# Attention: both heads' probabilities transposed together behind the scores, in two 64-row tiles

## What is computed

```python
x = x + tanh(g_xattn) * xattn(layernorm(x), ctx, ctx)
# xattn(q, k, v):
qh, kh, vh = split_heads(q @ Wq), split_heads(k @ Wk), split_heads(v @ Wv)
dots = where(mask | causal, -max, einsum('bhid,bhjd->bhij', qh, kh) * SCALE)
out = einsum('bhij,bhjd->bhid', softmax(dots), vh)
return merge_heads(out) @ Wo + bo
```

## Time and profile before

| what | value |
|---|---|
| median of 3 runs | 1721.62 us (1720.88 to 1722.0) |
| the profiled execution | 1721.11 us, span 1719.3 us |
| mean granted clock of PE | 0.982 of full speed |
| PE busy | 1641.4 us (95%), 13700 matmul records |
| DVE busy | 1354.0 us (79%) |
| ACT busy | 1157.7 us (67%) |
| POOL busy | 491.0 us (29%) |
| transposes of probabilities on PE (L792) | 1024, 160.3 us busy |
| exponentials on ACT (L428) | 1024, 396.9 us busy |

### The profile page before, as it was taken

How to read it: one execution, slowest core, us unless ns; L and a number is a source line. 1 busy time by engine, 2 the same in 40 slices (tenths; PEclk the granted TensorE clock), 3 DMA queues, 4 the chain that set the end, 5 groups by cost and what they waited for, 6 DMA issues and landing times. The chain is left out here.

```text
span 1719.3 us, 39257 instructions
## 1 busy us (share of the span) xinstructions
PE 1641.4 (95%) x13700; PEld 1371.8 (80%) x13700; DVE 1354.0 (79%) x2305; ACT 1157.7 (67%) x3047; POOL 491.0 (29%) x367
## 2 busy tenths in 40 slices
PE   8999999999999999999999999989997998886998
PEld 6788888888888888888888888778775777775887
DVE  7767778677686786777767768876887999898997
ACT  5666666566666665666666666557665999796665
POOL 2322323323232232232332323320001765560000
PEclk9999999999999999999999999998998999997999
DMA  4210001101010010100110001018994886564664
GB/s 140 70 40 27 24 26 37 38 26 37 14 50 24 26 37 25 39 24 26 37 38 26 24 26 37 14 62 250 332 320 179 300 295 230 214 251 172 214 220 152
DMA packets 74783, 177.18 MB, mean 103 GB/s; under 512 B 19312, under 2 KB 49136, under 8 KB 71792
## 3 DMA queue, kind: packets, MB, share of 16 engines
q1 hardware_dynamic: 74736, 176.57, 30.0%
HBM read 96.86 MB, written 76.02 MB: 101 GB/s over the span
## 5 line engine op out<-in xcount | busy, mean ns | idle before, releaser
L386 POOL TENSOR_TENSOR prob<-prob,rsums 128x512 f32<-128x512 f32 x254 | 266.9, 1051 | 785.0 <-DVE rsums L582 642.3
L428 ACT ACTIVATE prob<-masked,neg_max 128x128 f32<-128x128 f32 x1024 | 396.9, 392 | 77.6 <-DVE neg_max L560 76.7
L428 ACT ACTIVATION_READ_ACCUMULATOR prob<-masked,neg_max 128x1 f32 x1024 | 196.0, 191 | 0.0
L560 DVE TENSOR_REDUCE neg_max<-masked 128x4 f32<-128x512 f32 x254 | 174.4, 686 | 8.8
L578 DVE COPY probT<-trans 128x512 f32<-128x512 f32 x126 | 86.9, 690 | 110.0 <-PE trans L792 107.1
L558 DVE TENSOR_TENSOR masked<-score,mask_add 128x512 f32<-128x512 f32 x254 | 172.9, 681 | 0.8
L792 PE MATMUL trans<-ident,prob 128*128 128x128 f32 x1024 | 160.3, 279 | 0.8 <-POOL prob L406 0.8
L443 ACT ACTIVATE qT<-proj 128x512 f32<-128x512 f32 x128 | 76.7, 600 | 111.1 <-PE proj L757 111.1
L840 PE MATMUL y<-wo_hi,o_hi 128*128 128x256 f32 x508 | 145.9, 287 | 2.1 <-DVE wo_lo L508 2.0
L813 PEld LDWEIGHTS pv<-probT,v_sb 128*64 128x64 f32 x2048 | 109.7, 136 | 46.4 <-issue 44.4
L813 PE MATMUL pv<-probT,v_sb 128*64 128x128 f32 x2048 | 140.1, 279 | 6.6 <-issue 5.9
(11 more groups left out here) (251 smaller groups left out, 4386.5 us busy)
## 6 DMA issues: line engine op xcount, KB each, us to landing
gate<-gate_d SPq DMA_DIRECT2D x30, 768.0 KB, 4.3
n_x<-n_x_d SPq DMA_DIRECT2D x25, 512.0 KB, 5.0
gate_d<-stage SPq DMA_DIRECT2D x8, 1536.0 KB, 5.5
n_u_d<-w_raw SPq DMA_DIRECT2D x16, 768.0 KB, 4.0
stage<-n_u_d SPq DMA_DIRECT2D x16, 768.0 KB, 6.1
gate_d<-gate SPq DMA_DIRECT2D x7, 1536.0 KB, 5.5
x_in<-in_x SPq DMA_DIRECT2D x16, 512.0 KB, 4.0
ctx_in<-in_ctx SPq DMA_DIRECT2D x16, 512.0 KB, 3.5
```

The costliest lines, as they stand in the source:

```text
L386: gp.tensor_tensor(pr, pr, rsums[:, h, :].rearrange("p (b o) -> p b o", o=1).broadcast_to([P, NB, P]), ALU.mult).then_inc(normed, 1)
L428: nc.scalar.activation(prob[:, c % 2, h, b, :], masked[:, h, b, :], ACT.Exp, bias=neg_max[:, h, b:b + 1], accum_out=psums[:, h, b:b + 1]). ...
L560: nc.vector.tensor_reduce(neg_max[:, h, :], masked[:, h], X, ALU.max, negate=True).then_inc(max_done, 1)
```

## The change

Both heads' probabilities of a pair are transposed together, in front of the step's query product. Each 128x128 transpose becomes two: rows 0 to 63 of the probabilities go to the bank `trans`, rows 64 to 127 to the `proj` bank whose turn it is, so the turn is a new kind of job in `jobs`. One bank then holds half of the query rows of both heads, and ACT copies both banks, one after the other; DVE has no such copy any more. In steps 2 to 6 ACT takes both heads' exponentials before it copies the keys; in steps 0, 1 and 7 the order stays. DVE inverts the second head's sums right after the copies of the values. The feed-forward weights at the end have three banks in place of four.

```diff
+    V_JOBS = [(0, 1), (2, 3), (4,), (5,), (6,), (7,), (), ()]
     for c in range(NC):
-        jobs += [(c, "q", 0)]
+        jobs += [(c, "turn", 0), (c, "q", 0)]
...
 # ACT
+            K_COPY_FIRST = (0, 1, NC - 1)
+            def copy_turned(u, b, before):
+                act.wait_ge(transposed, u + 1)
+                wait(act, pv_done, u)
+                nc.scalar.activation(probT[:, :, :, 0:HALF], halves(hand.banks[0]), ACT.Copy).then_inc(first_copied, 1)
+                act.wait_ge(projected[b], before + 1)
+                nc.scalar.activation(probT[:, :, :, HALF:P], halves(proj[b]), ACT.Copy).then_inc(copied[b], 1)
...
                 if soft:
                     exps(u - 1, c + 1, 0)
+                    if c not in K_COPY_FIRST:
+                        exps(u - 1, c + 1, 1)
...
-                if soft:
+                if soft and c in K_COPY_FIRST:
                     exps(u - 1, c + 1, 1)
...
 # DVE
-                if old:
-                    dve.wait_ge(transposed, 2 * (u - 2) + 2)
-                    wait(dve, pv_done, u - 2)
-                    nc.vector.tensor_copy(probT[:, 1], trans[:]).then_inc(probT_copied[1], 1)
...
 # PE
+            def transpose_prob(u, c, b, before):
+                pe.wait_ge(normed, 2 * u + 2)
+                wait(pe, first_copied, u)
+                wait(pe, copied[b], before)
+                pe.nop(nofuse=True)
+                to = [halves(a) for a in (hand.banks[0], proj[b])]
+                for e in range(NB):
+                    for h in range(2):
+                        for r in range(2):
+                            rows = slice(r * HALF, (r + 1) * HALF)
+                            last = nc.tensor.transpose(to[r][:, h, e, :], prob[rows, c % 2, h, e, :], ident[rows, rows])
+                            if e == NB - 1 and h == 1:
+                                last.then_inc(projected[b] if r else transposed, 1)
...
                 if old:
-                    transpose_prob(u - 2, co, 0)
+                    transpose_prob(u - 2, co, *turn_bank(g, c, u))
...
-                if old:
-                    transpose_prob(u - 2, co, 1)
...
-        ffn_banks = [proj[0][:], proj[1][:]] + [a[:].rearrange("p b q -> p (b q)") for a in score]
+        ffn_banks = [proj[1][:]] + [a[:].rearrange("p b q -> p (b q)") for a in score]
```

More of the change, by code:

```diff
@@ L111, in jobs_of, with turn_job @@
         return [(i, n) for i, (cc, k, n) in enumerate(jobs) if cc == c and k == kind]
+    no_turn = [jobs.index((c, "turn", 0)) for c in range(2)]
+    no_input = [i for i, (_, kind, _) in enumerate(jobs) if kind == "t"]
     def nth(g, i):
-        skipped = KC // 2 if isinstance(g, int) and g == G - 1 and i == last_k else 0
-        return i % 2, (FIRST + i) // 2 + (NJ // 2) * g - skipped
+        left_out = [a for a in no_turn if not isinstance(g, int) or g > 0 or g == 0 and a < i]
+        if isinstance(g, int) and g >= G - 1:
+            left_out += [a for a in no_input if g == G or a < i]
+        return i % 2, (FIRST + i) // 2 + (NJ // 2) * g - sum(a % 2 == i % 2 for a in left_out)
+    def turn_job(u):
+        if not isinstance(u, int):
+            return None
+        if u >= U:
+            b, before = nth(G, 0)
+            return b, before + u - U
+        return nth(u // NC, jobs_of(u % NC, "turn")[0][0])
     with ExitStack() as st:
@@ L276, in w_part, with turn_bank @@
             return a[n][:].rearrange("p (k n) -> p k n", k=KC if n < 3 else 1)[:, :, lo:hi]
+        def turn_bank(g, c, u):
+            return turn_job(u) if isinstance(u, int) else nth(g, jobs_of(c, "turn")[0][0])
         def staged(i):
@@ L422, in exps @@
             def exps(u, c, h):
-                wait(act, transposed, 2 * (u - 2) + h + 1)
+                wait(act, transposed, u - 1)
                 act.wait_ge(max_done, 2 * u + h + 1)
@@ L434, in step @@
                 if old:
-                    act.wait_ge(transposed, 2 * (u - 2) + 1)
-                    wait(act, pv_done, u - 2)
-                    nc.scalar.activation(probT[:, 0], trans[:], ACT.Copy).then_inc(probT_copied[0], 1)
+                    copy_turned(u - 2, *turn_bank(g, c, u))
                 if new:
@@ L588, in step @@
                         nc.vector.tensor_copy(v_sb[:, n % NB, cols], proj[b][:]).then_inc(copied[b], 1)
+                if soft:
+                    dve.wait_ge(exp_done, NB * (2 * (u - 1) + 2))
+                    wait(dve, normed, 2 * (u - 1))
+                    nc.vector.reciprocal(rsums[:, 1, :], psums[:, 1, :]).then_inc(recip_done, 1)
                 if nxt:
@@ L801, in scores_free, with times_v @@
                     wait(pe, masked_done, 2 * (u - 1) + h + 1)
-            def times_v(u, c, then=None):
-                for h in range(2):
-                    pe.wait_ge(probT_copied[h], u + 1)
+            def times_v(u, c, b, before, then=None):
+                pe.wait_ge(first_copied, u + 1)
+                pe.wait_ge(copied[b], before + 1)
                 wait(pe, out_split, u)
@@ L884, in step @@
                 if nxt:
+                    transpose_in(g, *ts[2])
                     transpose_in(g, *ts[3])
                 if old:
-                    times_v(u - 2, co, (g, c, u) if new else None)
+                    times_v(u - 2, co, *turn_bank(g, c, u), (g, c, u) if new else None)
                 if new:
```

76 lines of the change are left out of this document (24 added, 52 removed).

## The result

The changed kernel takes 1790.57 us (median of 4 runs, 1786.75 to 1794.18), the kernel before 1721.25: the ratio is 1.0404 [1.0379, 1.0429]. The direction and its mechanism came as predicted. The range of 1742 to 1795 holds the time, but the forecast of 1761 was 30 us short. The profiled execution took 1792.12, its span 1790.3.

The account below looks back on a forecast made before the run. A step was taken to last as long as TensorE's matmuls, other engines having slack. Step changes of +38 and 2 at the end made +40 on 1721.1, forecasting 1761 us, range 1742 to 1795.

Parts of the forecast that it names:

- rival A: In the turn, the two row tiles do not overlap or weight loads set the pace: 1810 us, chance 0.13.
- The turn's price: On TensorE the tiled turn takes 0.64 us instead of 0.88, so a step with nobody late is 0.24 shorter.
- Steps 1 to 3: Loop steps where the turn waits 0.20 us for GpSimd's second multiplication against 0.24 saved: -0.04 each.
- Step 0: First loop step: the turn waits 0.86 us for GpSimd behind the second head's late exponentials: +0.62.
- Step 4: Loop step with late exponentials: eight stand before the keys' copy, so the next scores come later: +1.12 us.
- step 6: Loop step without a value product to hide the turn's wait; eight exponentials and the keys' copy delay scores: +0.91 us.
- Step 5: Loop step given time by the pushed-back one before it, the keys just fitting: -0.24 us.
- Step 7: Last loop step, held by ScalarE behind the second input transpose, before which the turn is 0.20 us longer: +0.20.
- The sum over the attention: All loop steps' changes over the 16 groups, added together: +38 us.
- The tail: End of the attention: two copies in a row and three feed-forward banks cost 0 to 3 us, taken as 2.
- Rival C: The keys' copies are not late in steps four and six but the waits stay: 1722 us, no difference, chance 0.05.
- Rival B: GpSimd's second multiplication ends before the scores in all steps and the keys fit: faster, 1690 us, chance 0.06.

## Why the prediction was right, and where it was off

- **What bounds.** Right: a step lasts as long as its matmuls until somebody is late, and the change makes two late. Alone, in the kernel before, the order of ScalarE costs 37 us; in the changed kernel the reciprocal's move gave back 25. No run undoes both, so that the two add up is not shown.
- **The range** holds the time by luck. Its part above 1780 stood for a part of rival A, a pair of transposes at 0.085; the pair came at 0.062. What filled the 30-odd us above the forecast was the term below on how late a result is taken up (17), the first and last groups (4), the tail (2) and the stages behind (8).
- **The turn's price** was right: 0.24 saved. The steps of 8.22 that have no wait show it, and with it the waits account for the others, to 0.05.
- **Steps 1 to 3** were put at -0.04 and came at +0.04, +0.14, +0.07. The step that failed is "TensorE takes up such a result 0.06 after its end", which I had read at one place, the end of the attention. In front of the turn it is 0.15, in step 2 0.24, and so the wait is 0.29 (0.39 in step 2) instead of 0.20. Why it differs is open: the new `transpose_prob` has one wait more and an empty instruction behind the wait for GpSimd, and no run takes them out.
- **Step 0**: +0.82 for +0.62, the same term. GpSimd ends 0.86 after the turn could have begun, foreseen as 0.80, and the release is 0.24.
- **Step 4**: +1.25 for +1.12, **step 6** +1.07 for +0.91. The chain is as written: exponentials, keys, last block, scores. From the end of the keys' copy to the scores it took 0.60, and 0.71 in the run of this order alone, where I had 0.43: the same 0.06 again, for ScalarE's copy. Why the exponentials of step 4 come late was read loosely: the 0.57 us sum began before GpSimd's add had ended, and no run tests whether the add holds it up. The sum used only their start.
- **Step 5**: -0.10 for -0.24. "The keys just fit" was 0.14 short, by the same term: their copy ends at 661.58 and the scores come 0.59 later. **Step 7**: +0.27 for +0.20.
- **The sum over the attention** was +38 and came to +58.6. The measured step lengths, at the counts of the prediction, make 17 of the 21 missing; the rest lies in the first and last groups.
- **The tail**, taken as 2, was 6.8 at the gate stage's first instruction and 3.8 by its second tile. The step that failed is the sentence that put the three banks at "between 0 and 3 (28 closing transposes of 0.11 come behind a later one)": it followed TensorE's order, not VectorE's, where the fourth low part stands behind the maxima, and it kept 0.11 for transposes behind a hole in which the granted clock fell.
- **"The later stages are not touched"**: no line is, yet they were 8.2 longer in the profile. That term was set to nothing without a row behind it, and its cause is open.
- **Rival A** is out by the order of rows: the tiles overlap. The argument against it from the loads was misread: only the first two of four whole transposes' loads start 0.06 apart. All four take 0.42 and one 0.14, so the other two distances are 0.11:

```profile
611.79 0.42 PEld L792 LDWEIGHTS trans<-ident,prob 128*128 128x128 f32 x4
...
628.26 0.14 PEld L811 LDWEIGHTS trans<-ident,prob 64*128 64x128 f32 x1
...
628.29 0.14 PEld L811 LDWEIGHTS proj<-ident,prob 64*128 64x128 f32 x1
```

  (The last two are of the changed kernel.) The Trainium skill's page "TensorE: Matmul & The Clock Gate", section "LDWEIGHTS (loading the stationary operand)", would have a load of 128 columns take 107 ns. The whole transposes' 0.11 agrees with it; in the turn the two 64-row tiles' loads of 128 columns start 0.03 apart (0.06 within a tile), so there the measurement decides against it. **Rival C** fell with its condition: the keys were late. **Rival B** did not come: GpSimd ends after the scores, because the change leaves the reciprocal behind the values' copy. Moved in front of it, the reciprocal does let the turn follow the scores in steps 1 to 4.
- **The rule on changing the tiling**: the Trainium skill's page "TensorEngine Tiling (Array Packing)", section "Tiling Modes", has a change drain the engine. The runs fit it: the same tiles that save 0.2 a step next to the scores save next to nothing between two full-array products.

## What to carry to other kernels

Work on the busiest engine that is moved to an earlier place saves its own time only if what it consumes is there by then: look for what released the producer (here a reciprocal behind a copy that had nothing to do with it), and price the release by several places of the trace, not by the shortest. When two consumers of one engine's output both sit without slack, an order that helps one takes from the other; then move the consumer behind work that covers it, and check that the added copy fits there. A bank taken away at a stage's end is paid where another engine's queue releases it, and, if TensorE idles for it, in its clock as well.

## What was not expected

- The same kind of release took 0.06 at one place, 0.15 or 0.24 from GpSimd in front of the turn, and 0.23 or 0.34 from ScalarE's copy of the keys.
- Two 64-row tiles with 64 moving columns give a pair every 0.062 us, and keep overlapping where the program lists one tile after the other: spread 0.76, not the 0.93 of 15 x 0.062.
- 5.42 us of nothing on TensorE are followed by 5.4 us at a granted clock of 0.59; 1.61 us of nothing, at the same place, by 1.00.
- Sixteen empty instructions on TensorE behind the turn lengthen no step: the medians of all eight are those of the run without them, to 0.01.
